# An RWKV-6 attention block with a routed feed-forward on one core: the pair levels of a unit in two TensorE visits instead of six, with copied keys and queries

## The reference, cut to what matters

```python
xn = layernorm(x)
# attention: five token-shift mixtures of xn and its predecessor, with low-rank learned terms
w, k, v, r, g = ...            # k = k_in @ Wk.T * exp(min(w, 0)); g = tanh(g_in @ Wg1) @ Wg2
def step(S, inp):              # per head of 64 channels, token after token
    rt, kt, vt, dt = inp       # dt = exp(w)
    kv = vt[..., :, None] * kt[..., None, :]
    yt = einsum('bnj,bnij->bni', rt, S + uu[..., None, :] * kv)
    S = S * dt[..., None, :] + kv
    return (S, yt)
attn = (groupnorm(y) * gamma + beta) * g @ Wo.T
# feed-forward: each token goes to the one of 8 experts with the largest probability
h = relu(tokens @ W1[e] + b1[e]);  ffn = (h @ W2[e] + b2[e]) * max_prob
out = x + attn + ffn
```

## Time and profile before

| | us |
|---|---|
| median of three runs | 612.1 |
| the profiled execution | 608.76 |
| its span, first to last instruction | 607.1 |
| TensorE busy | 555.6 (92%) |
| VectorE busy | 451.4 (74%) |
| ScalarE busy | 298.8 (49%) |
| GpSimd busy | 187.9 (31%) |
| mean granted TensorE clock | 0.989 of full |

### The profile page before, as it was taken

One profiled execution on the slowest core, in us unless ns is written; L12 is line 12 of the kernel. 1 busy time (PEld: TensorE's weight loads), 2 busy tenths in 40 slices (PEclk: granted clock), 3 DMA queues, 4 the chain that ended last, 5 costly groups with the idle time before them and its releaser, 6 DMA issues.

```text
span 607.1 us, 18589 instructions
## 1 busy us (share of the span) xinstructions
PE 555.6 (92%) x7278; PEld 483.7 (80%) x7278; DVE 451.4 (74%) x1124; ACT 298.8 (49%) x625; POOL 187.9 (31%) x148
## 2 busy tenths in 40 slices
PE   2778889988999999999999999999999999999884
PEld 2557677877898989898887889898789888788783
DVE  6979899988587786858676868768685867686722
ACT  4874273434535546463735364554446373535351
POOL 4401010121333342432433224325133343322523
PEclk9999798999999999999999999999999999999998
DMA  8979424599342243132432223432304243121423
GB/s 283 272 252 303 124 82 132 125 360 297 81 67 75 45 85 58 36 90 44 92 51 71 45 71 57 85 45 61 72 21 90 42 94 48 28 45 29 63 44 35
DMA packets 49799, 60.73 MB, mean 100 GB/s; under 512 B 5057, under 2 KB 44098, under 8 KB 49570
## 3 DMA queue, kind: packets, MB, share of 16 engines
q1 hardware_dynamic: 36898, 44.72, 25.8%
q0 software_dynamic: 11840, 14.42, 15.8%
q10 hardware_dynamic: 976, 0.41, 0.2%
HBM read 40.79 MB, written 23.07 MB: 105 GB/s over the span
## 4 chain that ended last, share of the span: by engine, by line
PE 70%; DVE 17%; issue 4%; DMA 3%; ACT 2%; SPq 2%; POOL 1%; ACTq 0%; DVEq 0%; POOLq 0%
PE F L642 12%; PE LL L521 8%; PE F L634 8%; PE G L457 8%; PE YB L610 4%; PE G L489 4%; PE YB L567 4%; PE G L426 4%; PE G L473 4%; PE YB L565 3%; DVE mix L1014 2%; DMA w<-in_W 2%; SPq L1825 2%; DVE small L813 2%; DVE mix L1022 2%
## 5 line engine op out<-in xcount | busy, mean ns | idle before, releaser
L1672 POOL DMA_INDIRECT out<-rows,dst_row x39 | 65.6, 1683 | 198.0 <-DVE rows L1136 187.2
L642 PE MATMUL F<-w,hsT 128*128 x312 | 76.3, 387 | 3.1 <-ACT hsT L1493 1.6
L634 PE MATMUL F<-xsT,w1s 128*128 128x128 f32 x624 | 76.7, 276 | 1.3 <-ACT xsT L1475 1.3
L634 PEld LDWEIGHTS F<-xsT,w1s 128*128 128x128 f32 x624 | 73.9, 192 | 2.6 <-ACT xsT L1475 1.6
L1014 DVE SCALAR_TENSOR_TENSOR mix<-G,vec,ba 128x256 f32<-128x256 f32 x160 | 69.5, 476 | 6.4 <-PE G L426 6.4
L1493 ACT ACTIVATE hsT<-F,b1c 128x128 f32<-128x128 f32 x156 | 44.6, 368 | 54.0 <-PE F L634 53.9
L1066 DVE TENSOR_TENSOR RK<-RK,D 128x256 f32<-128x256 f32 x112 | 51.5, 460 | 25.5 <-issue 24.2
L1050 DVE COPY_PREDICATED AP_<-msk,LL 128x256 f32<-128x256 uint32 x96 | 51.3, 534 | 25.3 <-PE LL L521 22.5
L642 PEld LDWEIGHTS F<-w,hsT 128*128 128x128 f32 x312 | 57.1, 190 | 11.9 <-issue 3.6
L521 PEld LDWEIGHTS LL<-RK 64*64 64x64 f32 x2560 | 45.9, 136 | 21.6 <-issue 17.1
L521 PE MATMUL LL<-RK 64*64 64x32 f32 x2560 | 54.5, 223 | 6.9 <-DVE D L1068 6.9
(11 more groups left out here) (171 smaller groups left out, 1098.0 us busy)
## 6 DMA issues: line engine op xcount, KB each, us to landing
cd<-cd_d SPq DMA_DIRECT2D x30, 320.0 KB, 5.5
w<-in_W SPq DMA_DIRECT2D x16, 512.0 KB
cd_d<-w SPq DMA_DIRECT2D x32, 160.0 KB, 2.7
b2t<-in_b SPq DMA_DIRECT2D x39, 128.0 KB
w<-in_x SPq DMA_DIRECT2D x8, 512.0 KB, 9.4
xn_d<-w SPq DMA_DIRECT2D x8, 512.0 KB
out<-in_x SPq DMA_DIRECT2D x8, 512.0 KB, 5.1
out<-res POOLq DMA_DIRECT2D x16, 256.0 KB, 4.6
```

The source lines that it names most:

```text
L634: i1 = pe.matmul(FB[:, k * P:(k + 1) * P], w1s[:, cc, k, :], xsT[:, cc, :], start=(cc == 0), stop=(cc == 1))
L642: i1 = pe.matmul(FB[:, 0:C], hsT[:, k, :], w2[:, bass.ds(number[f] * (HC * C) + k * C, C)], start=(k == 0), stop=(k == HC - 1))
L1672: pool.indirect_dma_start(io["out"], bass.IndirectOffsetOnAxis(dst_row[:, f:f + 1], 0), ys[:, f % 2, :], None, compute_op=ALU.add).then_in ...
```

## The change

- TensorE: `level` is called inside two new functions. `middle_levels` makes B = 2, 4 and 8 in one visit, `last_levels` the block and B = 16 and 32. The number of products is the same.
- B = 2, 4, 16 and 32 no longer read K and R, but copies of the needed halves. ScalarE makes them (`saved`, two copies of 128 x 256 for each of the four), into `Ru`, into the front of D and into the upper half of the other unit's `AT`. Their semaphore is `sv`.
- VectorE: `grow` and `level` are called apart, so that the multiplications run ahead of the copies out. `grow` of B = 2, 4, 16, 32 waits for `sv`, of 1 and 8 for the visit that still reads K and R.
- Orders of the first part, of `half` and of the end are new, on TensorE, VectorE and ScalarE; `gate_up`, `variance`, `affine` are earlier in a half. In ScalarE's half `block` goes ahead of `gate_down`; `spread` and `bonus` are the last two, behind `out` (in the last half they are earlier).
- Tiles: half 10 takes 3 instead of 2, so 3 are left for the end.
- SyncE: W2 is issued ahead of the first expert bias, with no wait for `ex` before it.
- The last unit's squares go to the mixture buffer.

```diff
-EACH = [0 if h == 0 else 2 if h % 3 == 1 and h != 4 else 3 for h in range(NU - 2)]
+EACH = [0 if h == 0 else 2 if h % 6 == 1 else 3 for h in range(NU - 2)]
...
+            def middle_levels(u, c):
+                q = seq(u, c)
+                pe.wait_ge(s["a"], NLEV * q + 2)
+                pe.wait_ge(s["sv"], NSAVE * q + 2)
+                pe.wait_ge(s["gr"], NGROW * q + 3)
+                saved_level(u, 2, 0)
+                saved_level(u, 3, LEAF // 2)
+                own_level(u, 4, WIDE).then_inc(s["lev"])
+
+            def last_levels(u, c):
+
+                q = seq(u, c)
+                pe.wait_ge(s["a"], NLEV * q + 5)
+                pe.wait_ge(s["sv"], NSAVE * (q + 1))
                 pe.wait_ge(s["gr"], NGROW * q + 6)
...
+                saved_level(u, 5, LEAF)
+                saved_level(u, 6, WIDE).then_inc(s["lev"])
...
@@ TensorE, half
                 key(u, c + 1)
                 if fb is not None:
                     tokens(fb)
-                level(*v, 2)
                 mixed(u, c + 1, 3)
+                gate_up(u, c)
                 value(u, c + 1)
                 if fb is not None:
                     hidden(fb)
-                level(*v, 3)
+                middle_levels(*v)
                 mixed(u, c + 1, 4)
-                receptance(u, c + 1)
-                level(*v, 4)
                 if fb is not None:
                     down(fb)
                 if fc is not None:
                     tokens(fc)
-                level(*v, 5)
-                gate_up(u, c)
+                receptance(u, c + 1)
                 if fc is not None:
                     hidden(fc)
-                level(*v, 6)
+                last_levels(*v)
                 gated_back(u, c)
                 gate_down(u, c + 1)
-                block(*v)
                 output(u, c)
...
@@ VectorE, half
-                levels(*v, 0, 1)
+                grow(*v, 1)
+                levels(*v, 0)
                 if fa is not None:
                     expert_out(fa)
+                grow(*v, 2)
                 key(u, c + 1)
-                levels(*v, 2)
+                levels(*v, 1)
+                variance(u, c)
                 mixed(u, c + 1, 3)
+                grow(*v, 4)
                 added(u, c + 1, 3)
-                variance(u, c)
-                levels(*v, 3)
                 normed(u, c)
+                affine(u, c)
+                grow(*v, 8)
                 mixed(u, c + 1, 4)
-                levels(*v, 4)
+                levels(*v, 2, 3)
+                grow(*v, 16)
                 if fb is not None:
                     expert_out(fb)
-                affine(u, c)
-                levels(*v, 5)
+                levels(*v, 4)
+                gated(u, c)
+                grow(*v, 32)
                 added(u, c + 1, 4)
-                gated(u, c)
-                levels(*v, 6)
-                grow(*v, 64, 6)
+                grow(*v, 64)
+                levels(*v, 5, 6)
...
@@ ScalarE
+            def saved(u, c, B):
+                q, n = seq(u, c), SAVED.index(B)
+                act.wait_ge(s["gr"], NGROW * q + (1, 2, 4, 8, 16, 32).index(B))
...
+                act.activation(ksv[u][n % 2].rearrange("p g (n h t) -> p g n h t", h=2, t=B)[:, :, :, 0, :],
+                               flat4(K[:, u]).rearrange("p (g n h t) -> p g n h t", n=LEAF // (2 * B), h=2, t=B)[:, :, :, 0, :], ACT.Copy)
+                act.activation(rsv[:, n % 2, :, :].rearrange("p g (n t) -> p g n t", t=B),
+                               flat4(R[:, u]).rearrange("p (g n h t) -> p g n h t", n=LEAF // (2 * B), h=2, t=B)[:, :, :, 1, :], ACT.Copy).then_inc(s["sv"])
...
@@ ScalarE, half
-                bonus(u, c + 1)
                 if fc is not None:
                     rectified(fc)
                 gated_back(u, c)
+                block(*v)
+                if h == NU - 3:
+                    bonus(u, c + 1)
                 gate_down(u, c + 1)
+                if h == NU - 3:
+                    spread(*v)
                 if fc is not None:
                     weights(fc + 1)
-                block(*v)
-                spread(*v)
                 out(u, c)
+                if h < NU - 3:
+                    spread(*v)
+                    bonus(u, c + 1)
...
@@ SyncE
-            sp.wait_ge(s["ex"], 1)
-            bias(0)
             sp.wait_ge(s["inv"], 1)
             for e in range(E):
                 sp.dma_start(w2[:, e * HC * C:(e + 1) * HC * C].rearrange("p (c n) -> p c n", c=HC),
                              io["W2"][e].rearrange("(c p) n -> p c n", p=P)).then_inc(s["ew2"], 16)
+            sp.wait_ge(s["ex"], 1)
+            bias(0)
```

More of the change, by code:

```diff
@@ L747, in tensor_program @@
             mixed(0, 1, 2)
-            codes(5)
             read_out(0, 0, 0)
             read_out(0, 0, 1)
+            codes(7)
             decay_up(0, 1)
-            first_levels(1, 0)
+            table(0)
             key(0, 1)
-            codes(6)
-            level(1, 0, 2)
             mixed(0, 1, 3)
+            table(1)
+            middle_levels(1, 0)
+            gate_up(0, 0)
             value(0, 1)
-            codes(7)
-            level(1, 0, 3)
             mixed(0, 1, 4)
+            table(2)
             receptance(0, 1)
-            table(0)
-            table(1)
-            level(1, 0, 4)
-            table(2)
             table(3)
-            level(1, 0, 5)
-            gate_up(0, 0)
-            level(1, 0, 6)
             gated_back(0, 0)
             gate_down(0, 1)
-            block(1, 0)
             output(0, 0)
+            last_levels(1, 0)
             for h in range(1, NU - 2):
@@ L778, in tensor_program @@
             tokens(LAST[0])
+            read_out(0, c, 0)
+            read_out(0, c, 1)
             hidden(LAST[0])
-            read_out(0, c, 0)
-            level(1, c, 2)
-            read_out(0, c, 1)
+            gate_up(0, c)
+            middle_levels(1, c)
             down(LAST[0])
-            level(1, c, 3)
             tokens(LAST[1])
-            gate_up(0, c)
-            level(1, c, 4)
             hidden(LAST[1])
-            level(1, c, 5)
+            last_levels(1, c)
+            gated_back(0, c)
             down(LAST[1])
-            gated_back(0, c)
             tokens(LAST[2])
-            level(1, c, 6)
+            read_out(1, c, 0)
+            read_out(1, c, 1)
             output(0, c)
             hidden(LAST[2])
-            block(1, c)
+            gate_up(1, c)
             down(LAST[2])
-            tokens(LAST[3])
-            read_out(1, c, 0)
-            read_out(1, c, 1)
-            hidden(LAST[3])
-            gate_up(1, c)
-            down(LAST[3])
             gated_back(1, c)
@@ L1510, in half @@
                 decay(u, c + 1)
+                saved(*v, 2)
                 if h == 1:
@@ L1519, in half @@
                     weights(fb + 1)
-                receptance(u, c + 1)
+                saved(*v, 16)
                 if fc is not None:
@@ L1523, in half @@
                     last_bias(fc)
-                bonus(u, c + 1)
+                saved(*v, 32)
+                receptance(u, c + 1)
                 if fc is not None:
@@ L1566, in scalar_program @@
             bonus(0, 0)
+            codes(2)
+            scaled(3)
             gate_down(0, 0)
-            codes(2)
+            saved(0, 0, 2)
+            saved(0, 0, 4)
+            codes(3)
             decay_down(1, 0)
-            scaled(3)
+            scaled(4)
             decay(1, 0)
+            saved(0, 0, 16)
+            saved(0, 0, 32)
+            codes(4)
+            scaled(5)
             value(1, 0)
-            codes(3)
-            scaled(4)
-            receptance(1, 0)
             act.wait_ge(s["z_pool"], 4)
             block(0, 0)
+            receptance(1, 0)
             bonus(1, 0)
+            codes(5)
+            scaled(6)
             gate_down(1, 0)
             spread(0, 0)
-            codes(4)
-            scaled(5)
             key_back(0, 0)
-            decay_down(0, 1)
-            codes(5)
-            scaled(6)
-            squares(0, 0)
-            decay(0, 1)
             codes(6)
             scaled(7)
+            decay_down(0, 1)
+            squares(0, 0)
+            codes(7)
+            decay(0, 1)
+            saved(1, 0, 2)
+            saved(1, 0, 4)
+            saved(1, 0, 16)
             value(0, 1)
-            codes(7)
             receptance(0, 1)
-            bonus(0, 1)
             gated_back(0, 0)
+            saved(1, 0, 32)
             gate_down(0, 1)
+            out(0, 0)
             act.wait_ge(s["z_pool"], 5)
@@ L1605, in scalar_program @@
             last_bias(LAST[0])
+            saved(1, c, 2)
+            saved(1, c, 4)
+            squares(0, c)
             rectified(LAST[0])
             weights(LAST[1])
-            squares(0, c)
+            saved(1, c, 16)
             tokens(LAST[1])
             last_bias(LAST[1])
+            saved(1, c, 32)
```

(12 more changed lines are left out.)

219 lines of the change are left out of this document (124 added, 95 removed).

## The result

| | before | after |
|---|---|---|
| median of 19 runs each, us | 611.44 (608.52 to 614.67) | 613.36 (611.19 to 619.47) |
| ratio after / before | | 1.0052 [1.0031, 1.0072] |
| profiled execution / its span, us | 608.76 / 607.1 | 612.62 / 611.3 |

The forecast was 605.8 us in 595 to 613, so the time lies 7.6 us above it and just outside the range. Which chip this comparison ran on is not recorded. Run once more later (e17, on a chip of its own), the same unedited kernel took 602.93 us against 607.81, a ratio of 0.9922 [0.9881, 0.9963]. That is the forecast, nearly. What differs between these two traces of one program is half of the answer.

What follows compares the result with a forecast made beforehand. TensorE bounds nine of thirteen halves, VectorE the first part, a chain the end. Terms +4.9 + 1.7 - 3.2 - 1.5 - 2.5 - 5.7 = -6.3 us gave 602.5 against 608.76 profiled, 605.8 us on the median; range 595 to 613.

Steps and rivals of the forecast that it cites:

- first part (loop begins): Stretch before half 1: VectorE's new order starts half 1's first mixture near 128.7, not 131.7; -2.5 us taken.
- loop: +4.9 +1.7 -3.2 -1.5: Half 1 to the end: nine three-tile halves +4.9, half 10's third tile +1.7, two-tile halves -3.2, W2 -1.5 us.
- end: After the last half: one tile less and six level visits in two, finishing at +40.2 against 45.9; -5.7 us.
- Boundary: Start of three-tile halves: ScalarE's queue, with `bonus` new there, delays the next `tokens`; TensorE stands still 1.2 us.
- The first rival: Boundary of halves: ScalarE reaches the next `tokens` by G + 6, dense half 32.6, whole 594 us; chance 0.22.
- Half of 33.8: Three-tile half: TensorE alone 32.6 us plus a boundary gap of 1.2, against 33.26 before.
- the price of long visits: TensorE's merged level visits: 32 records take 0.60 us, 19 ns each, so middle visit 1.80 and last 1.81.
- the rival that long runs of small products lose pace: TensorE's visits: 96 records in a row settle at 25 ns, 1.0 us more a half, 619 us; chance 0.08.
- The upper end of the range: Whole kernel, 613 us: first part at its upper bound, +5.5, and 0.2 per half for the copies.
- My bound of 3 us lost: First part's worst case: visits hold TensorE until ScalarE's copies are made, and 1.2 GHz stretches may move.
- W2: Half 1: earlier load of W2 removes the first `down`'s wait of 1.52 us; -1.5 us.
- Copies: ScalarE's saved copies, about 0.85 us a pair, are ready 0.4 to 1.0 before VectorE asks; price zero.

Runs made afterwards that it cites:

- e17: Changed kernel run once more without any edit, on a third chip without stops; 602.93 us, ratio 0.9922 to the kernel before.
- e2: Kernel before the change, with ScalarE's `bonus` moved behind `out` to the end of the half; 619.43 us, ratio 1.0206.
- e1: Changed kernel with ScalarE's `bonus` moved from the end of a half to behind the next half's `key_back`; 591.6 us, ratio 0.9738 to the kernel before.
- e12: Changed kernel with `bonus` behind the next `key_back`, the block last in the last visit, and `added` ahead of the seam's masked copies; 607.05 us, ratio 0.9935.
- e9: Changed kernel, half 1's first `mixed` and `added` ahead of the last two masked copies on VectorE, `key_back` ahead of `spread` on ScalarE; 613.31 us, ratio 1.0036.
- e4: Changed kernel with SyncE's W2 load held until all visits of the first two units are done; 609.86 us, ratio 1.0032.
- e14: Changed kernel with `bonus` behind the next half's `key_back`, the same edit as e1, on another chip; 596.32 us, ratio 0.9763.
- e15: Changed kernel with the first part's last visit ahead of `output`, `grow` 32 ahead of `experts_of_tiles`, `block` and `spread` ahead of `out`; 602.94 us, ratio 0.9892.
- e6: Changed kernel run again without any edit, on a chip with stops; 613.66 us, ratio 1.0041 to the kernel before.
- e7: Changed kernel with SyncE's first expert bias ahead of the W2 load again, as in the kernel before; 615.4 us, ratio 1.0059.
- e5: Changed kernel with `bonus` behind the next half's `key_back` and VectorE's `expert_out(fb)` ahead of `grow` 16; 597.64 us, ratio 0.9751.
- e13: Changed kernel with `bonus` behind the next `key_back` and VectorE's order behind mixed 4 rearranged, so two TensorE waits go; 589.02 us, ratio 0.9676.

## Why the prediction was wrong, by its own steps

| step, us | forecast | after | same kernel, e17 |
|---|---|---|---|
| first part (loop begins) | -2.5 | +3.5 | +1.3 |
| loop: +4.9 +1.7 -3.2 -1.5 | +1.9 | +6.1 | -1.5 |
| end | -5.7 | -5.4 | -5.4 |
| sum against the profiled run | -6.3 | +4.2 | -5.6 |

That e17 comes within 0.7 of the sum is in part luck: its first part is 3.8 worse than forecast and its loop 3.4 better.

**Boundary: right, and it is the lever.** A gap of 1.2 was forecast, 1.1 came (0.99 in the row), released by ScalarE's `xsT`, ten times. e2 puts such a gap into the old kernel, for 8 us; e1 and e12 take it out of the new one, for 11 us of loop each. The first rival ("does not cost", 594) falls as a forecast, yet it is what e1 reaches by one moved line.

**Half of 33.8: mis-sized both ways.** Without stops it is 33.45: the gap is 0.1 shorter, and TensorE alone gives 33.45 - 1.1 = 32.35 where I had 32.6. The two visits take 1.54 + 1.52 us there, forecast 1.80 + 1.81, so 0.55 less; a wait of 0.40 ahead of the third `hidden`, which I had not listed, takes most of that back. With stops the half is 33.99. A three-tile and a two-tile half together (first levels to first levels, 306.10 to 371.50 before) were 65.4 before, forecast 64.9, and came out at 65.4 after and 64.3 in e17.

**The step that failed is the price of long visits.** I costed them at 19 ns a record and gave 0.08 to the rival that long runs of small products lose pace, worth 1.0 a half and 619 us. Their pace is better than forecast: the 96 of the middle visit take 1.53 us, 16 ns each. What comes in its place is a full stop of 0.5 us behind 46 or 47 pairs of the last visit. Over thirteen halves that is 428.7 - 421.2 = 7.5 us, and the visit at the seam loses 2.2 more; the sum missed by 10.5. Without the 7.5 the loop would have been 3.4 better than forecast; with it, it is 4.2 worse and its gain against the kernel before becomes a loss. The upper end of the range had 0.2 us a half for the copies and the first part at its bound, and nothing for the visits. The 25 ns that this rival cites from the Trainium skill (TensorE: Matmul & The Clock Gate) stand in its section Wait — 56ns, not 53.3ns?, not in the one named.

**First part: -2.5 became +3.5 (+1.3 in e17).** I laid out VectorE's order and expected half 1's first mixture near 128.7 in place of 131.7; it came at 134.30 (133.44 in e17). The new order puts the last visit as TensorE's last work, and VectorE's chain (`grow` 64, two copies, `mixed`, `added`) starts only behind it. That wait I had not listed: 1.27 to 1.74. Taking 0.9 of it away (e9) moved neither clock nor time. `decay_down` begins 2.3 later than before (135.95 against 133.61), with 2.2 of stops in the visit ahead of it. From there to `first_levels` it is 6.08 us, at 1.2 GHz for half of it, against 4.92 before; that is the other 1.2. Without stops (e17) it is 1.5 later and then 4.72. One trace says little here: the loop begins between 138.5 and 147.7 in the eighteen traces of the new order, at 138.5 and 140.7 in the two of the old. In the eighteen traces of the new order the mean clock over 132 to 150 us was 1.00 in three, 0.91 in three and 0.81 or lower in twelve, among them all nine on chips with stops; the two of the old order had 1.00. Whether the seam's stops make the clock fall is not shown: e4, e14 and e15 have none and 0.72. Over its 19 executions the changed kernel took 4.1 us more for each 0.01 of mean clock, and beside each other (e6's chip) the means were 0.980 after and 0.985 before. My bound of 3 us lost was half a microsecond too small.

**W2: not shown.** The wait of 1.52 is gone, but e7, with W2 late again, has none either: issued half a microsecond later than in the kernel before, where W2 was there at 152.46, it is needed only at 154.40. And in the changed kernel the first `down` stands still behind its first product, which starts at 152.91, the second at 153.93; e7 and e17 have no such stop. What it is stays open. The end of a wait for a load is worth something only if its reader does not come later anyway.

**End: right** (-5.7, -5.4). **Copies: right**, no `grow` of the changed kernel's loop waits for them but one in half 1 of e17 (0.75), which TensorE does not feel. They stand behind the bias in ScalarE's queue, though, and there e4's late bias costs 1.82. **Cover of `hidden`**: the wait of 0.23 in the row, 0.40 by starts, is for VectorE's output of the tile before (`fy`); e5 and e13, which move that output, have none.

## What to carry to other kernels

When edits of a queue's end are moved about, write down what stands in front of the next stage's first producer: three short operations at the end of ScalarE's half cost 11 us here, 1.8% of the kernel, and moving one call gave them back. Time a result of half a percent on more than one chip before explaining it: the same program was 0.5% slower once and 0.8% faster another time, and a single row of the traces told most of the difference. Merging short visits of small products can have a price that the short ones do not show, so look for stops by the starts of the rows, not by their idle times.

## What the runs showed of the hardware

- Long runs of small products stop once in every last visit in nine traces of the new order, for about 0.5 us (0.3 in e5), and in nine more on three other chips they don't (no gap over 0.26), the same program among both. The two traces of the old order, whose visits are no longer than 32, have no such row; one of the two is from a chip without stops, and the chip of the other is not recorded.
- Small 64x64 products with 32 columns start 16 ns apart in a run of 96 (1.53 us), nearer than the 19 ns of the short visits. The Trainium skill (TensorE: Matmul & The Clock Gate, Wait — 56ns, not 53.3ns?) has about 25 ns as the closest; the traces here are below it.
- The granted clock differs between executions of one program by up to 0.018 in the mean (0.968 to 0.986 over 19), which is 8 us here.
